# GpSimd's order inside a chunk of phase 2: the sum of x and y2 goes first, the low half of block 6 goes ahead of the rebuilt y

## The chip, the cores and the metric

The kernel runs on one core of a Trainium2 chip. The metric is the device time of one execution in microseconds (us). The kernel before took 651.34 us (median of three runs, 648.35 to 652.54). TensorE is called PE below, VectorE DVE, ScalarE ACT, GpSimd POOL, and the engine that only issues transfers SP.

## The reference, cut to what matters

The input is 8192 rows of 256 numbers (2 sequences of 4096). Two layers follow each other, each behind a layer norm and with a residual.

```
y   = _layernorm(x)
h   = y + linear_attention(_layernorm(y)*g1+b1, wq, wk, wv) @ wo     # y2 in the kernel
h   = h + lookup_act((_layernorm(h)*g2+b2) @ w1) @ w2                # w1: 256x1024, w2: 1024x256
x   = x + h                                                          # xp in the kernel
out = x + (_layernorm(x) @ CB.T) * (SCB/127) + bias
```

lookup_act rounds its argument to steps of 0.1 and takes the GELU of the rounded value.

## The kernel before

The rows are worked off in 16 chunks of 512 (each held as 128 partitions x 4 rows x 256). Phase 1 (up to about 204 us) runs over all chunks and leaves the key-value sums and phi(q). Phase 2 runs over the chunks again and does the rest; the change lies there. Every matmul operand in fp32 is split into a rounded "high" part and a "low" part (the rest), which are multiplied one after the other.

Each engine has its own instruction stream, written by hand, and the streams meet at semaphores. Nothing is scheduled by a tool. In phase 2 each stream is a function `body(i, ...)` that mixes work of neighbouring chunks: `main` is the MLP of chunk i, `prv` what is left of chunk i - 1 (its xp, its norm n3, the product with CB, the output), `nxt` what has to be ready for chunk i + 1 (its attention output, y2, norm n2), `nn` work for chunk i + 2.

What each engine does in a chunk, in the order of its stream:

- PE (`body`, L1133): up 0, up 1 (products with w1, blocks of 128 of the 1024 columns), turn of the attention, up 2, up 3, down 0 (product with w2, needs high and low part of block 0), attention_out (with wo), down 1, up 4, turn of n3 (needs `n3_ready`), down 2, up 5, down 3, up 6, the product with CB, turn of n2 (`turn2`, needs `n2_ready`), up 7, down 4, the first half of the attention of chunk i + 2, down 5, down 6, its second half, down 7.
- ACT (`body`, L556): for each block of up a rounding to int8 (L540), GELU into `tf` (L548) and GELU into the high part `t_hi` (L550, signals `t_hi_ready`). Between them the high parts of the turned tiles (L494 and L503). The GELU of block m waits until the low part of block m - 2 has read `tf`.
- DVE (`body`, L772): xp = PSUM + xz (L778), the statistics of xp (L615), low part of the attention (L745), mean and variance (L622), low part of block 1 (L738), n3 (`normalise`, four instructions at L729), low of block 3, y2 of chunk i + 1 (L755), its statistics, the low part of turned n3 (L745), n2 of chunk i + 1 (L729 again), ot (L802), low of block 5 (L738), low part of turned n2 (L768), attention of chunk i + 2 first half (L712 to L719), low of block 7 (L738), second half of the attention.
- POOL (`body`, L345): low parts of the even blocks (`mlp_low`, one instruction at L343, signals `t_lo_p`), the powers for n3 and n2 (`power`, L322 and L324), xz = x + y2 of chunk i (L355, waits for `xp_ready` of chunk i - 1 since xp reads the old xz), y of chunk i + 2 rebuilt from x (`first_norm`, L330 and four at L336), xb = xp + bias (L367) and the output ot + xb (L372).

SP reads x of chunk i + 2 once xz of chunk i is done (`xz_ready`), and writes an output once `out_ready` says so.

Of the kernel before, what the change touches and what calls it, by code (L numbers as in the profile page):

```python
# [24 lines left out]
ALU = mybir.AluOpType  # L25
# [19 lines left out]
def wait(eng, sem, value):  # L45

    if isinstance(value, int) and value <= 0:
        return
    eng.wait_ge(sem, value)
# [8 lines left out]
def build(nc, x, ln1_g, ln1_b, wq, wk, wv, wo, ln2_g, ln2_b, w1, w2, cb, scb, bias, out):  # L58
# [15 lines left out]
    with ctx:  # L74
# [3 lines left out]
        def sem(name):  # L78
            return ctx.enter_context(nc.semaphore(name))
# [57 lines left out]
        x2 = [take(CE) for _ in range(2)]  # L137
        take(CE)
        xz, xp, xb, ot = (take(CE) for _ in range(4))
# [3 lines left out]
        yb, at_, y2, nt = (take(CE) for _ in range(4))  # L143
# [44 lines left out]
        s = {n: sem(n) for n in names}  # L188
# [9 lines left out]
        def tm(a):  # L198

            return a.rearrange("p (j d) -> p j d", j=TT)  # L200
# [71 lines left out]
        def _(g):  # L272
# [46 lines left out]
            def power(c, u, r, mv, ready, arg, done):  # L319
                wait(g, s[ready], c + 1)  # L320
                hold(g, s["held_pool"])
                nc.gpsimd.tensor_scalar(u[:, :], mv[:, 1:2 * TT:2], 1.0, EPS, ALU.mult, ALU.add).then_inc(s[arg], 1)  # L322
                g.wait_ge(s[arg], c + 1)
                nc.gpsimd.tensor_tensor(r[:, :], u[:, :], minus_half[:, 0:TT], ALU.pow).then_inc(s[done], 1)  # L324

            def first_norm(c, p, turn):

                wait(g, s["y_ready"], c)
                hold(g, s["held_pool"])
                nc.gpsimd.tensor_copy(st2[:, :], chunk(stats_all, c, 2 * TT)).then_inc(s["stats_now"], 1)  # L330
                g.wait_ge(s["stats_now"], c + 1)
                g.wait_ge(x2_loaded[p], turn * 16 + 16)
                wait(g, s["y2_ready"], c)
                hold(g, s["held_pool"])
                for j in range(TT):
                    i = nc.gpsimd.tensor_scalar(tm(yb)[:, j], tm(x2[p])[:, j], st2[:, j:j + 1], st2[:, TT + j:TT + j + 1],  # L336
                                                ALU.mult, ALU.add)
                i.then_inc(s["y_ready"], 1)

            def mlp_low(c, m):  # L340
                n = c * (MT // 2) + m // 2
                wait(g, s["t_hi_ready"], c * MT + (m + 1))
                nc.gpsimd.tensor_tensor(t_lo[m % SLOTS], tf[m % 2], t_hi[m % SLOTS].bitcast(F32), ALU.subtract).then_inc(s["t_lo_p"], 1)  # L343

            def body(i, p, turn, prv, main, nxt, nn):  # L345

                if main:
                    mlp_low(i, 0)
                if prv:
                    power(i - 1, u3, r3, mv3, "mv3_ready", "u3_ready", "pow3")  # L350
                if main:

                    wait(g, s["xp_ready"], i)
                    g.wait_ge(s["y2_ready"], i + 1)
                    nc.gpsimd.tensor_tensor(xz, x2[p], y2, ALU.add).then_inc(s["xz_ready"], 1)  # L355
                    mlp_low(i, 2)
                if nxt:
                    power(i + 1, u2, r2, mv2, "mv2_ready", "u2_ready", "pow2")
                if main:
                    mlp_low(i, 4)  # L360
                if nn:
                    first_norm(i + 2, p, turn + 1)
                if main:
                    mlp_low(i, 6)
                if prv:
                    wait(g, stored, i * 16)
                    nc.gpsimd.tensor_tensor(tm(xb), tm(xp), bias_b.unsqueeze(1).to_broadcast([P, TT, D]),  # L367
                                            ALU.add).then_inc(s["xb_ready"], 1)
                if prv:
                    g.wait_ge(s["ot_ready"], i + 2)  # L370
                    g.wait_ge(s["xb_ready"], i + 2)
                    nc.gpsimd.tensor_tensor(xb, ot, xb, ALU.add).then_inc(s["out_ready"], 1)  # L372
# [23 lines left out]
            nc.gpsimd.tensor_scalar(scb_b, scb_b, 1.0 / 127.0, 0.0, ALU.mult, ALU.add).then_inc(s["scb_scaled"], 1)  # L396
            g.wait_ge(loaded["bias"], 16)
            body(0, 0, 0, False, True, True, True)
            body(1, 1, 0, True, True, True, True)
            with g.Fori(1, CHUNKS // 2 - 1) as it:  # L400
                for p in range(2):
                    body(it * 2 + p, p, it, True, True, True, True)
# [868 lines left out]
```

## Time and profile before

| | |
|---|---|
| median of three runs | 651.34 us |
| the profiled execution, its own time | 651.4 us |
| its span, first to last instruction | 649.6 us |
| outside the span | 1.8 us |
| phase 2 begins (chunk 0's first products) | about 204 us |
| xp of chunk 0 to xp of chunk 13 (13 chunks) | 227.27 to 582.47 us |
| DVE, ACT, POOL busy over the span | 80%, 63%, 59% |
| mean of one ACT instruction at L540, L548, L550 | 681, 632, 619 ns |

Times in the trace are counted from the start of the span. A row of the timeline gives the start, the length, the engine, the line, what is written from what, how many instructions are merged into the row, and in brackets how long the engine sat idle just before and what ended that. A chunk is followed below from the start of DVE's xp (L778), called xp + 0. PE's matmul ends are modelled, so starts are the better marks on PE.

### The profile page before, as it was taken

How to read it: one execution, taken by the hardware profiler on the slowest of the kernel's cores; microseconds unless marked ns; L12 is line 12 of the kernel's file. 1: busy time of each engine (PE TensorE's matmuls, PEld its weight loads, DVE VectorE, ACT ScalarE, POOL GpSimd, SP SyncE). 2: the span in 40 equal slices, each digit the busy share in tenths (PEclk: the TensorE clock that was granted, in tenths of full speed). 3: DMA queues.
4: the chain of work that ended last, by engine and by line, in shares of the span. 5: the costliest groups of instructions: out<-in, count | busy, mean ns of one | idle time of the engine just before them, and what ended most of it. 6: DMA issues, size and time to landing. Idle time of an engine off the chain costs nothing.

```text
span 649.6 us, 12205 instructions
## 1 busy us (share of the span) xinstructions
PE 586.2 (90%) x3838; PEld 517.6 (80%) x3838; DVE 517.0 (80%) x1076; ACT 411.7 (63%) x767; POOL 386.2 (59%) x337
## 2 busy tenths in 40 slices
PE   6999999999997999898998989989899898998875
PEld 6887787878786878788787978879788797887675
DVE  5488988898873688878888788887988878888656
ACT  2377767676765685675756757576665766657560
POOL 3446475655542447676486765757657576675553
PEclk8599999999997999999999999999999999999898
DMA  8101112021101000000100001010110000100001
GB/s 287 53 34 65 59 38 65 32 65 34 66 1 36 17 32 33 32 32 32 65 32 32 33 33 65 32 32 32 32 65 32 32 32 32 65 24 11 33 1 67
DMA packets 11128, 29.16 MB, mean 45 GB/s; under 512 B 2016, under 2 KB 4576, under 8 KB 11104
## 3 DMA queue, kind: packets, MB, share of 16 engines
q1 hardware_dynamic: 9472, 28.32, 12.3%
q10 hardware_dynamic: 1632, 0.53, 0.4%
q8 instruction: 15, 0.25, 0.2%
q14 instruction: 9, 0.07, 0.0%
HBM read 20.45 MB, written 8.39 MB: 44 GB/s over the span
## 4 chain that ended last, share of the span: by engine, by line
PE 36%; DVE 27%; issue 16%; POOL 12%; ACT 6%; DMA 1%; DVEq 1%; ACTq 0%; POOLq 0%; SPq 0%
PE psum L914 31%; DVE f_arena L729 8%; POOL f_arena L355 5%; DVE bn_stats L615 5%; PE psum L932 4%; POOL rstd L324 3%; DVE f_arena L755 3%; DVE f_arena L657 2%; DVE mean_var L622 2%; ACT grid_index L540 2%; DVE f32r_arena L738 2%; POOL pow_arg L322 2%; ACT f32r_arena L550 2%; ACT f32r_arena L494 1%; DVE f_arena L642 1%
## 5 line engine op out<-in xcount | busy, mean ns | idle before, releaser
L914 PE MATMUL psum<-w_hi,f32r_arena 128*128 128x256 f32 x1280 | 178.7, 286 | 5.1 <-DVE f32r_arena L738 3.5
L914 PEld LDWEIGHTS psum<-w_hi,f32r_arena 128*128 128x128 f32 x1280 | 164.9, 190 | 16.0 <-issue 11.5
L914 PE MATMUL psum<-f32r_arena,w_hi 128*128 128x512 f32 x512 | 143.0, 411 | 3.7 <-issue 3.7
L540 ACT ACTIVATE grid_index<-psum,w_bias_in_steps 128x512 int8<-128x512 f32 x128 | 87.2, 681 | 69.9 <-PE psum L914 69.9
L729 DVE TENSOR_SCALAR f_arena<-f_arena,mean_var,rstd 128x256 f32<-128x256 f32 x124 | 102.7, 887 | 25.9 <-POOL rstd L324 25.9
L914 PE MATMUL psum<-f32r_arena 128*128 128x512 f32 (+1 forms) x512 | 120.5, 378 | 2.6 <-issue 1.5
L343 POOL TENSOR_TENSOR f32r_arena<-f_arena,f32r_arena 128x512 fp32r<-128x512 f32 x64 | 86.0, 1344 | 56.3 <-ACT f32r_arena L550 56.3
L914 PEld LDWEIGHTS psum<-f32r_arena,w_hi 128*128 128x128 f32 x512 | 91.1, 194 | 22.4 <-ACT grid_index L540 4.7
L932 PE MATMUL psum<-ident,f_arena 128*128 128x128 f32 x504 | 69.6, 283 | 36.9 <-DVE f_arena L729 32.3
L932 PEld LDWEIGHTS psum<-ident,f_arena 128*128 128x128 f32 x504 | 58.6, 145 | 52.1 <-issue 28.3
L914 PEld LDWEIGHTS psum<-f32r_arena 128*128 128x128 f32 x512 | 83.2, 190 | 14.9 <-issue 3.1
L548 ACT ACTIVATE f_arena<-grid_index 128x512 f32<-128x512 int8 x128 | 80.9, 632 | 16.0 <-POOL f32r_arena L343 10.7
L550 ACT ACTIVATE f32r_arena<-grid_index 128x512 fp32r<-128x512 int8 x128 | 79.2, 619 | 0.0
L322 POOL TENSOR_SCALAR pow_arg<-mean_var 128x4 f32<-128x4 f32 x31 | 10.4, 334 | 97.5 <-DVE mean_var L622 97.4
L657 DVE SCALAR_TENSOR_TENSOR f_arena<-f_arena 128x256 f32<-128x256 f32 x64 | 46.4, 733 | 18.4 <-ACT f_arena L473 17.8
L738 DVE TENSOR_TENSOR f32r_arena<-f_arena,f32r_arena 128x512 fp32r<-128x512 f32 x64 | 51.8, 810 | 7.4 <-ACT f32r_arena L550 7.4
L745 DVE TENSOR_TENSOR f32r_arena<-psum,f32r_arena 128x512 fp32r<-128x512 f32 x62 | 39.5, 679 | 22.3 <-ACT f32r_arena L494 22.3
L494 ACT ACTIVATE f32r_arena<-psum 128x512 fp32r<-128x512 f32 x62 | 33.5, 595 | 31.9 <-PE psum L932 31.9
L285 POOL TENSOR_SCALAR pow_arg<-mean_var 128x4 f32<-128x4 f32 x16 | 8.3, 520 | 69.4 <-DVE mean_var L622 69.4
L615 DVE BATCH_NORM_STATS2 bn_stats<-f_arena 128x6 f32<-128x256 f32 x128 | 44.9, 414 | 4.7 <-DMA f_arena<-in_L_attn_x_dram 4.2
L914 PEld LDWEIGHTS psum<-f_arena 128*128 128x128 f32 x260 | 36.2, 192 | 15.6 <-DVE f_arena L657 12.9
L914 PE MATMUL psum<-f_arena 128*128 128x129 f32 (+1 forms) x260 | 41.6, 288 | 5.5 <-DVE f_arena L657 4.8
(96 smaller groups left out, 976.4 us busy)
## 6 DMA issues: line engine op xcount, KB each, us to landing
f_arena<-in_L_attn_x_dram SPq DMA_DIRECT2D x32, 512.0 KB, 3.3
out_dram<-f_arena SPq DMA_DIRECT2D x15, 512.0 KB, 2.6
f_arena<-in_L_attn_w_dram SPq DMA_DIRECT2D x2, 1024.0 KB, 11.3
out_dram<-f_arena SPq DMA_DIRECT2D x2, 256.0 KB, 2.2
phi_q<-in_L_attn_wk_dram ACTq DMA_DIRECT2D x1, 256.0 KB, 4.9
phi_q<-in_L_attn_wv_dram ACTq DMA_DIRECT2D x1, 256.0 KB, 5.4
phi_q<-in_L_attn_wq_dram SPq DMA_DIRECT2D x1, 256.0 KB, 5.7
phi_q<-in_L_ffn_CB_dram SPq DMA_DIRECT2D x1, 256.0 KB, 7.8
```

Of the source, the lines that this page charges most:

```text
L343: nc.gpsimd.tensor_tensor(t_lo[m % SLOTS], tf[m % 2], t_hi[m % SLOTS].bitcast(F32), ALU.subtract).then_inc(s["t_lo_p"], 1)
L494: act(fm(dst)[:, k], bank(b + k), ACT.Copy).then_inc(s[done], 1)
L540: act(k8[:, m % 2], bank(AB + m % 2), ACT.Identity, scale=1.0 / STEP, bias=h_bias[:, m:m + 1]).then_inc(s["grid_ready"], 1)
L548: act(tf[m % 2], k8[:, m % 2], ACT.Gelu_apprx_tanh, scale=STEP)
L550: act(t_hi[m % SLOTS], k8[:, m % 2], ACT.Gelu_apprx_tanh, scale=STEP).then_inc(s["t_hi_ready"], 1)
L615: i = ve.bn_stats(scratch[:, 6 * j:6 * j + 6], tm(src)[:, j])
L657: ve.scalar_tensor_tensor(out=phi_k[j], in0=e_k[j % 2], scalar=1.0, in1=relu_k[j % 2], op0=ALU.min, op1=ALU.add).then_inc(s["phi_k_done"], 1)
L729: i = ve.tensor_scalar(tm(nt)[:, j], tm(src)[:, j], mv[:, 2 * j:2 * j + 1], r[:, j:j + 1], ALU.subtract, ALU.mult)
L738: ve.tensor_tensor(t_lo[m % SLOTS], tf[m % 2], t_hi[m % SLOTS].bitcast(F32), ALU.subtract).then_inc(s["t_lo_v"], 1)
L745: ve.tensor_tensor(fm(lo_)[:, k], bank(b + k), fm(hi_)[:, k].bitcast(F32), ALU.subtract).then_inc(s[done], 1)
L914: return nc.tensor.matmul(out_, lhs, rhs, start=start, stop=stop, skip_group_check=True)
L932: i = nc.tensor.transpose(bank(b + k)[:, j * P:(j + 1) * P], tm(src)[:, j, k * P:(k + 1) * P], ident[:, :])
```

## The change

Only POOL's stream in phase 2 changes, and only in the order of its instructions. No instruction is added or taken away, no operand and no semaphore is changed.

- xz of chunk i moves from behind the power of n3 to the head of the chunk, in front of the low part of block 0. It keeps its wait for xp of chunk i - 1 (`xp_ready`), so the low part of block 0 and the power of n3 now stand behind that wait.
- The low part of block 6 moves ahead of `first_norm(i + 2)`, which keeps its own waits. The low parts of blocks 4 and 6 now follow each other.
- The power of n3 is followed by the low part of block 2, where it was followed by xz.

```
             def body(i, p, turn, prv, main, nxt, nn):
                 if main:
+                    wait(g, s["xp_ready"], i)
+                    g.wait_ge(s["y2_ready"], i + 1)
+                    nc.gpsimd.tensor_tensor(xz, x2[p], y2, ALU.add).then_inc(s["xz_ready"], 1)
                     mlp_low(i, 0)
                 if prv:
                     power(i - 1, u3, r3, mv3, "mv3_ready", "u3_ready", "pow3")
                 if main:
-                    wait(g, s["xp_ready"], i)
-                    g.wait_ge(s["y2_ready"], i + 1)
-                    nc.gpsimd.tensor_tensor(xz, x2[p], y2, ALU.add).then_inc(s["xz_ready"], 1)
                     mlp_low(i, 2)
                 if nxt:
                     power(i + 1, u2, r2, mv2, "mv2_ready", "u2_ready", "pow2")
                 if main:
                     mlp_low(i, 4)
+                if main:
+                    mlp_low(i, 6)
                 if nn:
                     first_norm(i + 2, p, turn + 1)
-                if main:
-                    mlp_low(i, 6)
```

Place 1 is POOL at the head of the loop over chunks. `f32r_arena<-f_arena,f32r_arena 128x512` is a low part, `f_arena<-f_arena 128x1024` at L355 or L351 is xz, and the two rows with `pow_arg` are the power of n3.

```order
 L400 ISA
+L350 REGISTER_ALU [waits xp_ready]
+L351 TENSOR_TENSOR f_arena<-f_arena 128x1024 [waits y2_ready]
+L49 ISA
 L343 TENSOR_TENSOR f32r_arena<-f_arena,f32r_arena 128x512 [waits t_hi_ready]
 L322 TENSOR_SCALAR pow_arg<-mean_var 128x4 [waits mv3_ready]
 L324 TENSOR_TENSOR rstd<-pow_arg,minus_half 128x4 [waits u3_ready]
-L354 REGISTER_ALU [waits xp_ready]
-L355 TENSOR_TENSOR f_arena<-f_arena 128x1024 [waits y2_ready]
 L49 REGISTER_ALU
 L343 TENSOR_TENSOR f32r_arena<-f_arena,f32r_arena 128x512 [waits t_hi_ready]
```

xz with its two waits has moved over block 0's low part and over the power.

Place 2 is the second half of the same chunk on POOL, from block 4's low part to the output. Before:

```order
L343 TENSOR_TENSOR f32r_arena<-f_arena,f32r_arena 128x512 [waits t_hi_ready]
L330 ISA [waits y_ready]
L330 COPY ln_scale_shift_now<-ln_scale_shift 128x8
L331 REGISTER_ALU
L332 ISA [waits stats_now]
L336 TENSOR_SCALAR f_arena<-f_arena,ln_scale_shift_now 128x256 [waits loaded_x2_0,y2_ready]
L336 TENSOR_SCALAR f_arena<-f_arena,ln_scale_shift_now 128x256 x3
L49 REGISTER_ALU
L343 TENSOR_TENSOR f32r_arena<-f_arena,f32r_arena 128x512 [waits t_hi_ready]
L49 REGISTER_ALU
L367 TENSOR_TENSOR f_arena<-f_arena 128x1024 [waits stored]
L372 TENSOR_TENSOR f_arena<-f_arena 128x1024 [waits xb_ready,ot_ready]
```

The same place now:

```order
L343 TENSOR_TENSOR f32r_arena<-f_arena,f32r_arena 128x512 [waits t_hi_ready]
L49 REGISTER_ALU
L343 TENSOR_TENSOR f32r_arena<-f_arena,f32r_arena 128x512 [waits t_hi_ready]
L330 ISA [waits y_ready]
L330 COPY ln_scale_shift_now<-ln_scale_shift 128x8
L331 REGISTER_ALU
L332 ISA [waits stats_now]
L336 TENSOR_SCALAR f_arena<-f_arena,ln_scale_shift_now 128x256 [waits loaded_x2_0,y2_ready]
L336 TENSOR_SCALAR f_arena<-f_arena,ln_scale_shift_now 128x256 x3
L49 REGISTER_ALU
L367 TENSOR_TENSOR f_arena<-f_arena 128x1024 [waits stored]
L372 TENSOR_TENSOR f_arena<-f_arena 128x1024 [waits xb_ready,ot_ready]
```

The second low part (block 6) has moved over the copy and the four instructions of y; xb (L367) now follows y directly.

## Rows read from the trace of the kernel before

**Rows 1.** The page, engines: busy us, share of the span, instructions.
```profile
PE 586.2 (90%) x3838; PEld 517.6 (80%) x3838; DVE 517.0 (80%) x1076; ACT 411.7 (63%) x767; POOL 386.2 (59%) x337
```

**Rows 2.** Windows, 13 chunks: stretch, length, busy and count by engine, clock, DMA.
```profile
227.27:582.47 355.20, 326.70 (x2290) 293.35 (x2289) 296.72 (x586) 235.21 (x403) 237.37 (x208) 1.00 0.10 37
```

**Rows 3.** Waits, 228 to 592 us: who waited, for whom, sum, times, longest.
```profile
PE psum L932 <- DVE f_arena L729: 27.6, 26, 1.6
```

**Rows 4.** Timeline of PE in one chunk, 337 to 365 us.
```profile
340.80 1.11 PE L914 MATMUL psum<-w_hi,f32r_arena 128*128 128x256 f32 x8
...
348.17 1.09 PE L932 MATMUL psum<-ident,f_arena 128*128 128x128 f32 x8 [1.54 <-DVE f_arena L729]
...
355.87 1.09 PE L932 MATMUL psum<-ident,f_arena 128*128 128x128 f32 x8 [0.66 <-DVE f_arena L729]
...
362.32 1.19 PE L914 MATMUL psum<-w_hi,f32r_arena 128*128 128x256 f32 x8
```

**Rows 5.** Timeline of DVE in the same chunk.
```profile
336.46 1.22 DVE L778 TENSOR_TENSOR f_arena<-psum,f_arena 128x1024 f32<-128x1024 f32 x1
337.71 1.41 DVE L615 BATCH_NORM_STATS2 bn_stats_b<-f_arena 128x6 f32<-128x256 f32 x4
...
341.42 0.37 DVE L622 BATCH_NORM_AGGREGATE mean_var<-bn_stats_b 128x2 f32<-128x6 f32 x4
...
343.70 4.34 DVE L729 TENSOR_SCALAR f_arena<-f_arena,mean_var,rstd 128x256 f32<-128x256 f32 x4 [1.27 <-POOL rstd L324]
...
353.37 2.44 DVE L729 TENSOR_SCALAR f_arena<-f_arena,mean_var,rstd 128x256 f32<-128x256 f32 x4 [0.45 <-POOL rstd L324]
...
361.25 0.68 DVE L738 TENSOR_TENSOR f32r_arena<-f_arena,f32r_arena 128x512 fp32r<-128x512 f32 x1
```

**Rows 6.** Timeline of POOL in the same chunk.
```profile
339.19 1.29 POOL L343 TENSOR_TENSOR f32r_arena<-f_arena,f32r_arena 128x512 fp32r<-128x512 f32 x1 [2.08 <-ACT f32r_arena L550]
341.99 0.50 POOL L322 TENSOR_SCALAR pow_arg<-mean_var 128x4 f32<-128x4 f32 x1 [1.50 <-DVE mean_var L622]
342.57 1.02 POOL L324 TENSOR_TENSOR rstd<-pow_arg,minus_half 128x4 f32<-128x4 f32 x1
343.56 2.39 POOL L355 TENSOR_TENSOR f_arena<-f_arena 128x1024 f32<-128x1024 f32 x1
345.91 1.33 POOL L343 TENSOR_TENSOR f32r_arena<-f_arena,f32r_arena 128x512 fp32r<-128x512 f32 x1
...
353.23 1.29 POOL L343 TENSOR_TENSOR f32r_arena<-f_arena,f32r_arena 128x512 fp32r<-128x512 f32 x1
...
354.96 2.36 POOL L336 TENSOR_SCALAR f_arena<-f_arena,ln_scale_shift_now 128x256 f32<-128x256 f32 x4 [0.24 <-POOL ln_scale_shift_now L330]
...
358.97 2.40 POOL L367 TENSOR_TENSOR f_arena<-f_arena 128x1024 f32<-128x1024 f32 x1
```

**Rows 7.** Timeline of ACT in the same chunk: block 2's high part, block 6's rounding.
```profile
342.93 0.61 ACT L550 ACTIVATE f32r_arena<-grid_index 128x512 fp32r<-128x512 int8 x1
...
353.14 0.67 ACT L540 ACTIVATE grid_index<-psum,w_bias_in_steps 128x512 int8<-128x512 f32 x1
```

**Rows 8.** Timeline, POOL, DVE and PE at the end of chunk 14.
```profile
606.17 2.35 POOL L372 TENSOR_TENSOR f_arena<-f_arena 128x1024 f32<-128x1024 f32 x1
606.94 2.12 DVE L738 TENSOR_TENSOR f32r_arena<-f_arena,f32r_arena 128x512 fp32r<-128x512 f32 x1 [0.93 <-ACT f32r_arena L550]
609.21 1.26 PE L914 MATMUL psum<-w_hi,f32r_arena 128*128 128x256 f32 x8 [2.57 <-DVE f32r_arena L738]
610.51 1.23 DVE L778 TENSOR_TENSOR f_arena<-psum,f_arena 128x1024 f32<-128x1024 f32 x1 [1.45 <-PE psum L914]
```

**Rows 9.** Timeline of PE in chunk 15, the turn of n3.
```profile
621.32 1.09 PE L932 MATMUL psum<-ident,f_arena 128*128 128x128 f32 x8 [2.48 <-DVE f_arena L729]
```

**Rows 10.** Lines L615 and L802, 228 to 595 us: count, shortest/median/longest ns.
```profile
L615 DVE BATCH_NORM_STATS2 bn_stats_b<-f_arena x56: 408/410/428, 228.5 to 584.7; 128x6 f32<-128x256 f32 x56
L802 DVE TENSOR_TENSOR f_arena<-psum,f_arena x13: 1205/1206/1214, 246.5 to 574.3; 128x1024 f32<-128x1024 f32 x13
```

More of the change, by code:

```diff
@@ L347, in body @@
                 if main:
+                    wait(g, s["xp_ready"], i)
+                    g.wait_ge(s["y2_ready"], i + 1)
+                    nc.gpsimd.tensor_tensor(xz, x2[p], y2, ALU.add).then_inc(s["xz_ready"], 1)
                     mlp_low(i, 0)
@@ L351, in body @@
                 if main:
-                    wait(g, s["xp_ready"], i)
-                    g.wait_ge(s["y2_ready"], i + 1)
-                    nc.gpsimd.tensor_tensor(xz, x2[p], y2, ALU.add).then_inc(s["xz_ready"], 1)
                     mlp_low(i, 2)
@@ L360, in body @@
                     mlp_low(i, 4)
+                if main:
+                    mlp_low(i, 6)
                 if nn:
                     first_norm(i + 2, p, turn + 1)
-                if main:
-                    mlp_low(i, 6)
                 if prv:
```

## The prediction

> **What bounds the kernel now.** I read the engines on the page first: PE is busy 90% of the span and no other engine over 80% [rows 1]. The windows view gives the repeating part. From xp of chunk 0 to xp of chunk 13 it takes 355.20 us for 13 chunks, 27.32 us each, at a granted clock of 1.00 [rows 2]. PE is busy 326.70 / 13 = 25.13 of those 27.32, so some 2.2 us a chunk are there to be won from it. The waits view says where they are: PE's turns of normalised tiles wait for DVE's normalise (L729) 27.6 us in 26 waits [rows 3]. In one chunk these are 1.54 us ahead of the turn of n3 and 0.66 us ahead of that of n2 [rows 4].
>
> The first is made by POOL. DVE's four instructions of n3 take 4.34 us, those of n2 2.44 us, for the same work on the same shapes [rows 5]. n3 starts at 343.70, when POOL has been in xz (2.39 us) for 0.14 us, and behind xz comes block 2's low part (1.33 us) [rows 6]. n2 starts 0.14 us into a low part of 1.29 us [rows 5, 6] and loses only about that. So a `normalise` instruction does not run while a POOL instruction does; it waits for its end. Chunk 14 shows the same for DVE's low part (L738). Block 7's starts at 606.94, 0.77 us into POOL's output instruction, which ends at 608.52, and ends itself at 609.06, 0.54 later; it takes 2.12 us [rows 8] where it takes 0.68 in the steady chunk [rows 5]. PE waits 2.57 us for it [rows 8].
>
> **The change, step by step.** All times from xp + 0 = 336.46.
>
> *Head of the chunk.* xp ends at 1.22 [rows 5]. POOL follows a DVE signal after about 0.2 (L622 ends 341.79, L322 starts 341.99) [rows 5, 6], so xz runs 1.42 to 3.8. Its old cover is gone: block 0's low part, which ran from 2.73 (339.19), now runs 3.8 to 5.1. PE's down 0 started at 4.34 (340.80) [rows 4]; with 0.1 for the signal it starts at 5.2. **Cost: 0.86 us of PE.** Behind down 0 on PE stands everything up to down 7. The power of n3 is not delayed: it waits for L622, which is ready at 5.33, and it started at 5.53 anyway [rows 5, 6].
>
> *n3.* The power ends at 7.13 [rows 6]. Block 2's high part is there at 7.08 (342.93 + 0.61) [rows 7], so the low part of block 2 runs from about 7.15 to 8.45, and n3 starts into it 0.1 us after its start. That is exactly the case of n2: 2.44 us in place of 4.34. n3 ends at 9.7 in place of 11.6, **1.9 us earlier**. PE gets to the turn of n3 at 5.83 us after down 0 (348.17 - 1.54 - 340.80) [rows 4], so at 11.0: it no longer waits. DVE's y2, its statistics, the power of n2, block 4's low part and n2 all move up by 1.9: low 4 ends at 16.15 (354.52 before), n2 at 17.45 [rows 5, 6]. PE is at the turn of n2 12.87 us after down 0 (355.87 - 340.80 - 1.54 - 0.66) [rows 4], at 18.1: no wait either. Up to here PE has won 2.20 and paid 0.86, **1.34 us a chunk**.
>
> *Second half.* Block 6's low part stands right behind block 4's, but its high part is not there. ACT rounds block 6 at 16.68 (353.14) [rows 7]; the rounding follows the turn of n3, so it comes 5.2 + (353.14 - 340.80 - 1.54) = 16.0 now. Three ACT instructions of 0.68, 0.63 and 0.62 us later it is 17.9. POOL waits from 16.15 and runs low 6 from 17.9 to 19.25. Then y: from the end of low 4 (354.52) to the end of L336 (357.32) it took 2.8 us [rows 6]. DVE's low part of block 5 asks for its turn at about 19.2 too; if it gets in first, POOL starts 0.6 later. So y ends at 22.05 to 22.65 and xb (2.40) at 24.45 to 25.05. Before, xb ended at 361.37, 24.9: the 1.9 us won by n3 are spent waiting for block 6.
>
> *What is late next.* Block 7's low part on DVE started at 361.25 [rows 5], 20.45 us after down 0; without the two PE waits 18.25, so it now starts at 5.2 + 18.25 = 23.45. That is inside xb. Before, it came 0.12 us ahead of xb's end and lost nothing. Now it waits for xb's end and takes 0.54 more, as in chunk 14: it ends at 25.0 to 25.6. PE, which would be ready for down 7 at 5.2 + (362.32 - 340.80 - 2.20) = 24.5 [rows 4], starts it 0.15 after that (609.06 to 609.21), at 25.15 to 25.75. The next xp comes 1.30 after down 7 (609.21 to 610.51) [rows 8]: the chunk takes 26.45 to 27.05 us. I take the middle, **26.75, or 0.57 us less a chunk**. POOL's output instruction then ends near 27.6, 0.9 behind the next xp and ahead of the 1.42 at which the next xz could start, so it adds nothing.
>
> Here a rule can be set beside the rows. The Trainium skill, page "SBUF — State Buffer", section "Who interferes with whom", says that a DVE instruction with two SBUF inputs contends with a GpSimd instruction that reads SBUF, and that who issues first holds the shared ports for the whole instruction. By that rule L738 pays for xb in full, as the row of 606.94 has it; without it the chunk would take the 25.8 of the first rival.
>
> *The ends.* Chunk 0 has no n3; I take nothing there. In chunk 14 there is no y, so xb starts at 19.25 to 19.85 and the output ends near 24.0 to 24.6; block 7's low part then ends at 24.5 to 25.1 and down 7 starts at 24.7 to 25.3 behind that chunk's xp (582.47), before at 26.74 [rows 8]: 1.4 to 2.0, take 1.6. In chunk 15 the turn of n3 waits 2.48 us [rows 9], because POOL stood at block 0's low part with xz still to come; with xz done while it waits, n3 loses one short instruction: 1.9 of the 2.48.
>
> *Transfers.* The read of x for chunk i + 2 hangs on xz and starts some 6 us earlier, the write of the output where it did. Nothing waits for either.
>
> **Sum.** 13 x 0.57 = 7.4, plus 1.6, plus 1.9: 10.9 us. The profiled execution took 651.4 us (span 649.6 and 1.8 around it), the median of three runs is 651.34: there is no difference to carry over. 651.4 - 10.9 = **640.5 us**. With 26.45 and 27.05 us a chunk and both ends of chunk 14 it is 636 to 645.
>
> **Rivals.**
>
> 1. *Block 7's low part escapes xb.* This happens if POOL's y ends later than 23.45 (0.8 to 1.4 us later than worked out), or if block 7's low part does not wait for an xb already running. Then down 7 starts at 24.5, the next xp at 25.8, and 13 x 1.52 = 19.8 plus 3.5 give **628 us**. Against it stands the row of 606.94. Chance 0.15.
>
> 2. *All is given back at xb.* y took 2.8 us in the chunk shown; every instruction of it that meets DVE adds up to 0.55. With 0.5 us more there and low 5 first, y ends at 23.15, xb at 25.55, and the chunk takes 25.55 + 0.54 + 0.15 + 1.30 = 27.5. 13 x 0.2 us are lost against 3.5 won at the ends: **650.5 us**, no change. Chance 0.2.
>
> 3. *Slower: xz and the statistics of xp get into each other's way.* xz now runs from 1.42, over DVE's L615 (337.71 to 339.12, four instructions) [rows 5]. If these wait like L729 does, one waits for xz (2.4) and one for low 0 (1.3). The two L745 behind them move from 3.75 to some 5.9, the attention's low part is there at 7.2 where PE wants it at 6.1, and mean and variance at 7.5. Everything from attention_out on is 1.2 later, the chunk takes 27.95, and the ends win 1.2 less each: 651.4 + 8.2 - 1.1 = **658.5 us**. It decides from the point at which down 0 and what follows are 0.6 later than worked out. Against it: L615 takes 408 to 428 ns in all 56 cases, but none of those had POOL beside it, so it is a gap and no proof. The nearest case, L802, reads one SBUF tile and PSUM while POOL is in y, and takes 1205 to 1214 ns throughout [rows 10]. Chance 0.08.
>
> For the third rival the same page and section of the Trainium skill has a rule: a DVE instruction with at most one SBUF input and outside the two-port modes does not contend with GpSimd. L802 agrees with it; for L615 no run here shows it yet. By the rule the third rival costs nothing and the 640.5 stand.
>
> **How the numbers follow.** The forecast (26.45 to 27.05 us a chunk, 636 to 645) has 0.52, the rivals 0.15, 0.2 and 0.08, and 0.05 is left for what I have not seen. The range takes in the first two rivals and leaves out the third: 626 to 651 us. A difference under 1% (644.9 to 657.9) can hardly be told from no change by a measurement of this kernel. Faster by over 1%: the forecast but for its upper edge (0.49), the first rival and a little of the rest, 0.66. Within 1%: 0.24. Slower: 0.1.
>
> **What the profile after would show.** Right: the first L729 row of a chunk takes 2.44 in place of 4.34; PE has no wait ahead of the turn of n3, but 0.6 us ahead of down 0 for POOL's L343, and 1 us or so ahead of down 7 for DVE's L738; that L738 takes 1.5 to 2.2 us; POOL waits 1.7 us for ACT ahead of block 6's low part. Wrong: if L738 stays at 0.68 there (first rival), if L615 grows beyond 0.43 (third), or if down 0 starts later than 5.3 behind xp. The forecast also falls if the order of PE's waits is not what I think, above all if n2 is late after all.

## The result and the profile after

| | before | changed |
|---|---|---|
| median | 650.99 us (4 runs, 648.35 to 652.54) | 633.17 us (4 runs, 631.93 to 634.82) |
| ratio | | 0.973, 95% interval 0.969 to 0.977 |
| span of the profiled execution | 649.6 us | 632.0 us |
| xp of chunk 0 | 227.27 | 223.34 |
| 13 chunks, xp 0 to xp 13 | 355.20 us, 27.32 each | 343.39 us, 26.41 each |
| chunk 14, xp to xp | 28.04 us | 26.96 us |
| from xp of chunk 14 to the end | 39.10 us | 38.34 us |

The kernel is 17.8 us faster; 10.9 were forecast. 633.2 us lies inside the stated range of 626 to 651 us, but below the 636 to 645 us of the forecast itself. Of the 17.6 us between the two profiled spans 11.8 lie in the 13 chunks, 1.1 in chunk 14, 0.8 behind it, and 3.9 ahead of the first xp, where the change touches almost nothing.

These are the rows of the changed kernel that answer to [rows 4 to 7]; the chunk shown begins with xp at 328.99. First PE: down 0, the turns of n3 and n2, down 7.

```profile
333.99 1.23 PE L914 MATMUL psum<-w_hi,f32r_arena 128*128 128x256 f32 x8 [0.38 <-POOL f32r_arena L343]
...
339.82 1.03 PE L932 MATMUL psum<-ident,f_arena 128*128 128x128 f32 x8
...
346.35 1.09 PE L932 MATMUL psum<-ident,f_arena 128*128 128x128 f32 x8
...
354.10 1.19 PE L914 MATMUL psum<-w_hi,f32r_arena 128*128 128x256 f32 x8 [1.04 <-DVE f32r_arena L738]
```

Both waits ahead of the turns are gone. Two others stand there: 0.38 us ahead of down 0 and 1.04 us ahead of down 7. DVE in the same chunk: xp, n3, n2, the low part of block 7, the next xp.

```profile
328.99 1.23 DVE L778 TENSOR_TENSOR f_arena<-psum,f_arena 128x1024 f32<-128x1024 f32 x1 [0.19 <-PE psum L914]
...
336.36 2.34 DVE L729 TENSOR_SCALAR f_arena<-f_arena,mean_var,rstd 128x256 f32<-128x256 f32 x4 [1.27 <-POOL rstd L324]
...
344.01 2.28 DVE L729 TENSOR_SCALAR f_arena<-f_arena,mean_var,rstd 128x256 f32<-128x256 f32 x4 [0.43 <-POOL rstd L324]
...
351.73 2.23 DVE L738 TENSOR_TENSOR f32r_arena<-f_arena,f32r_arena 128x512 fp32r<-128x512 f32 x1
...
355.42 1.22 DVE L778 TENSOR_TENSOR f_arena<-psum,f_arena 128x1024 f32<-128x1024 f32 x1 [0.18 <-PE psum L914]
```

n3 takes 2.34 us in place of 4.34, and block 7's low part 2.23 in place of 0.68. POOL in the same chunk: xz, low 0, the power of n3, low 2, low 4, low 6, y, xb and the output.

```profile
330.29 2.39 POOL L351 TENSOR_TENSOR f_arena<-f_arena 128x1024 f32<-128x1024 f32 x1 [0.52 <-DVE f_arena L778]
332.64 1.29 POOL L343 TENSOR_TENSOR f32r_arena<-f_arena,f32r_arena 128x512 fp32r<-128x512 f32 x1
...
335.24 1.02 POOL L324 TENSOR_TENSOR rstd<-pow_arg,minus_half 128x4 f32<-128x4 f32 x1
336.28 1.29 POOL L343 TENSOR_TENSOR f32r_arena<-f_arena,f32r_arena 128x512 fp32r<-128x512 f32 x1
...
343.87 1.30 POOL L343 TENSOR_TENSOR f32r_arena<-f_arena,f32r_arena 128x512 fp32r<-128x512 f32 x1
346.75 1.29 POOL L343 TENSOR_TENSOR f32r_arena<-f_arena,f32r_arena 128x512 fp32r<-128x512 f32 x1 [1.59 <-ACT f32r_arena L550]
...
348.88 2.18 POOL L336 TENSOR_SCALAR f_arena<-f_arena,ln_scale_shift_now 128x256 f32<-128x256 f32 x4 [0.24 <-POOL ln_scale_shift_now L330]
351.03 2.38 POOL L367 TENSOR_TENSOR f_arena<-f_arena 128x1024 f32<-128x1024 f32 x1
353.56 2.66 POOL L372 TENSOR_TENSOR f_arena<-f_arena 128x1024 f32<-128x1024 f32 x1
```

Block 7's low part asks at 351.73, 0.70 us into xb, which ends at 353.41; it ends itself at 353.96, 0.55 later. The waits view over 228 to 580 us says the same of all chunks (13 or 14 of each), where [rows 3] stood before:

```profile
PE psum L914 <- DVE f32r_arena L738: 13.4, 13, 1.2
...
PE psum L914 <- POOL f32r_arena L343: 5.9, 14, 0.6
```

No wait of PE's turns for L729 is left on PE's own row.

### The profile page after: what moved, and what is told of

The parts are those of the page before. It is cut to its first block, busy times and chain, and to the rows that moved or that the text cites. A ratio compares the mean times of both kernels' runs of the same rounds, so it can differ in the third digit from the quotient of the medians.

```text
span 632.0 us, 12211 instructions
## 1 busy us (share of the span) xinstructions
PE 579.8 (92%) x3838; PEld 514.7 (81%) x3838; DVE 504.9 (80%) x1076; ACT 411.3 (65%) x767; POOL 380.4 (60%) x337
## 4 chain that ended last, share of the span: by engine, by line
PE 37%; DVE 23%; POOL 17%; issue 15%; ACT 5%; DMA 1%; DVEq 1%; POOLq 0%; ACTq 0%; SPq 0%
PE psum L914 32%; PE psum L932 5%; DVE f32r_arena L738 4%; POOL f_arena L351 3%; DVE bn_stats L615 3%; POOL f32r_arena L343 3%; DVE f_arena L657 3%; POOL f_arena L372 3%; POOL f_arena L367 2%; DVE f_arena L729 2%; DVE f_arena L642 2%; POOL f_arena L336 2%; DVE f32r_arena L768 2%; POOL rstd L324 2%; DVE f_arena L755 1%
## 5 line engine op out<-in xcount | busy, mean ns | idle before, releaser
L914 PEld LDWEIGHTS psum<-f32r_arena,w_hi 128*128 128x128 f32 x512 | 89.6, 191 | 23.3 <-ACT grid_index L540 5.5
L343 POOL TENSOR_TENSOR f32r_arena<-f_arena,f32r_arena 128x512 fp32r<-128x512 f32 x64 | 83.0, 1297 | 35.9 <-ACT f32r_arena L550 35.4
L729 DVE TENSOR_SCALAR f_arena<-f_arena,mean_var,rstd 128x256 f32<-128x256 f32 x124 | 71.2, 634 | 25.7 <-POOL rstd L324 25.7
L738 DVE TENSOR_TENSOR f32r_arena<-f_arena,f32r_arena 128x512 fp32r<-128x512 f32 x64 | 69.1, 1080 | 7.5 <-ACT f32r_arena L550 7.4
L932 PEld LDWEIGHTS psum<-ident,f_arena 128*128 128x128 f32 x504 | 59.6, 145 | 14.8 <-DVE f_arena L642 3.9
L657 DVE SCALAR_TENSOR_TENSOR f_arena<-f_arena 128x256 f32<-128x256 f32 x64 | 49.3, 780 | 14.3 <-ACT f_arena L473 13.7
L745 DVE TENSOR_TENSOR f32r_arena<-psum,f32r_arena 128x512 fp32r<-128x512 f32 x62 | 39.5, 679 | 24.1 <-ACT f32r_arena L494 24.1
L615 DVE BATCH_NORM_STATS2 bn_stats<-f_arena 128x6 f32<-128x256 f32 x128 | 44.9, 413 | 4.8 <-DMA f_arena<-in_L_attn_x_dram 4.3
L351 POOL TENSOR_TENSOR f_arena<-f_arena 128x1024 f32<-128x1024 f32 x16 | 38.2, 2389 | 16.1 <-DVE f_arena L778 14.9
```

What stands on the lines that cost most here:

```text
L615: i = ve.bn_stats(scratch[:, 6 * j:6 * j + 6], tm(src)[:, j])
L657: ve.scalar_tensor_tensor(out=phi_k[j], in0=e_k[j % 2], scalar=1.0, in1=relu_k[j % 2], op0=ALU.min, op1=ALU.add).then_inc(s["phi_k_done"], 1)
L729: i = ve.tensor_scalar(tm(nt)[:, j], tm(src)[:, j], mv[:, 2 * j:2 * j + 1], r[:, j:j + 1], ALU.subtract, ALU.mult)
L738: ve.tensor_tensor(t_lo[m % SLOTS], tf[m % 2], t_hi[m % SLOTS].bitcast(F32), ALU.subtract).then_inc(s["t_lo_v"], 1)
L745: ve.tensor_tensor(fm(lo_)[:, k], bank(b + k), fm(hi_)[:, k].bitcast(F32), ALU.subtract).then_inc(s[done], 1)
L914: return nc.tensor.matmul(out_, lhs, rhs, start=start, stop=stop, skip_group_check=True)
```

## The experiments

Each line of an experiment's kernel stands one or two lower or higher than in the changed kernel (L777 or L779 is xp, L737 or L739 the low part on DVE, L728 or L730 n3 and n2, L349 xz where it stands at the head). Times per chunk are from xp of chunk 0 to xp of chunk 13 in the profiled execution, divided by 13. e1 to e4 ran on one chip, e5 to e8 on a second, e9 to e11 on a third. POOL's order in a chunk, in short:

| kernel | POOL's order | us a chunk | median us |
|---|---|---|---|
| before | low0 pow3 **xz** low2 pow2 low4 y low6 xb out | 27.32 | 651 |
| changed | xz low0 pow3 low2 pow2 low4 **low6 y** xb out | 26.41 | 633.2 |
| e1 | xz low0 pow3 low2 pow2 low4 y low6 xb out | 25.52 | 620.4 |
| e2 | low0 pow3 xz low2 pow2 low4 low6 y xb out | 28.16 | 661.0 |
| e3 | xz low0 pow3 low2 pow2 low4 low6 xb y out | 25.79 | 625.2 |
| e5 | low0 xz pow3 low2 pow2 low4 y low6 xb out | 26.19 | 632.5 |
| e7 | xz low0 pow3 low2 (n3) xb pow2 low4 low6 out y | 25.35 | 618.2 |
| e8 | low0 xz pow3 low2 (n3) xb pow2 low4 low6 out y | 26.09 | 629.5 |
| e9 | as e7 without the wait for n3 | 27.28 | 649.5 |

"(n3)" is a wait for DVE's n3.

### The two halves apart

e1_xz_only takes the move of block 6's low part back out of the changed kernel:

```
                     mlp_low(i, 4)
-                if main:
-                    mlp_low(i, 6)
                 if nn:
                     first_norm(i + 2, p, turn + 1)
+                if main:
+                    mlp_low(i, 6)
```

> Half of the change: xz at the head of the chunk, the low part of block 6 back behind y (first_norm). Theory A (a VectorE instruction with two SBUF inputs waits for the GpSimd instruction that is running, so block 7's low part pays for xb): with y right behind block 4's low part (16.2 us behind xp) y ends at 19.0, low 6 at 20.3, xb at 22.7 to 23.1. Block 7's low part asks at 22.7, so it loses at most 0.4 us where the changed kernel lost 1.5 (2.23 us in place of 0.68). PE's wait of 1.04 us ahead of down 7 goes, a chunk takes 25.4 to 25.7 in place of 26.43, 13 chunks win 10 to 13 us: 620 to 624 us. Rival B (the tail of the chunk is set by PE's own work and the wait at down 0, and block 6's low part is needed early): PE waits for the late low 6 ahead of down 6 instead, a chunk takes 26.4 or more, 633 us or above.

Measured: 620.4 us (618.22 to 625.84), 13 us less than the changed kernel. All 13 chunks took 25.3 to 25.5 us but one of 27.28. PE has no wait for L737 in the others. So this half alone brings more than both together, and the move of low 6 costs 13 us (10 us by the second measurement of e1's kernel, below).

The one slow chunk begins at 374.59. Of its end, first POOL (low 6, xb, output), then DVE (low 5, low 7):

```profile
393.29 1.29 POOL L343 TENSOR_TENSOR f32r_arena<-f_arena,f32r_arena 128x512 fp32r<-128x512 f32 x1
394.53 2.85 POOL L366 TENSOR_TENSOR f_arena<-f_arena 128x1024 f32<-128x1024 f32 x1
397.53 2.34 POOL L371 TENSOR_TENSOR f_arena<-f_arena 128x1024 f32<-128x1024 f32 x1
```

```profile
393.25 1.88 DVE L737 TENSOR_TENSOR f32r_arena<-f_arena,f32r_arena 128x512 fp32r<-128x512 f32 x1
...
397.64 2.78 DVE L737 TENSOR_TENSOR f32r_arena<-f_arena,f32r_arena 128x512 fp32r<-128x512 f32 x1
```

Low 5 begins 0.04 us ahead of low 6, and yet DVE waits here for POOL's whole low 6. Low 7 then comes 0.11 us behind the start of the output and waits for the rest of its 2.34 us. In the chunk ahead the same two met the other way round (low 5 at 367.91 took 0.79, POOL's low 6 from 368.13 took 1.72), and low 7 took 0.86. In the other 25 chunks (13 in each of this kernel's two profiles) low 5 was 0.06 us or more ahead and went first: a few hundredths of a microsecond decide over 1.9 us.

e2_low6_only keeps that move and puts xz back behind the power of n3:

```
                 if main:
-                    wait(g, s["xp_ready"], i)
-                    g.wait_ge(s["y2_ready"], i + 1)
-                    nc.gpsimd.tensor_tensor(xz, x2[p], y2, ALU.add).then_inc(s["xz_ready"], 1)
                     mlp_low(i, 0)
                 if prv:
                     power(i - 1, u3, r3, mv3, "mv3_ready", "u3_ready", "pow3")
+                if main:
+                    wait(g, s["xp_ready"], i)
+                    g.wait_ge(s["y2_ready"], i + 1)
+                    nc.gpsimd.tensor_tensor(xz, x2[p], y2, ALU.add).then_inc(s["xz_ready"], 1)
                 if main:
                     mlp_low(i, 2)
```

> The other half: block 6's low part ahead of y, xz where it was before (behind the power of n3). Theory A: n3 still takes 4.34 us behind xz and low 2, low 4 ends at 18.1 behind xp, low 6 waits for its high part and ends at 20.6, y at 23.4 to 24.0, xb at 25.8 to 26.4. Block 7's low part asks at 24.8, waits for xb and ends at 26.3 to 26.9; a chunk takes 27.8 to 28.4 in place of 27.32: 657 to 665 us, slower than before. Rival B: the earlier low 6 costs nothing and saves nothing, 27.3 us a chunk, 651 us.

Measured: 661.0 us, ratio to before 1.016 (1.010 to 1.022); 28.16 us a chunk. Slower than before by 1 to 2%, as theory A had it. DVE, n3 and the low part of block 7:

```profile
343.46 4.35 DVE L728 TENSOR_SCALAR f_arena<-f_arena,mean_var,rstd 128x256 f32<-128x256 f32 x4 [1.26 <-POOL rstd L324]
...
360.85 1.91 DVE L737 TENSOR_TENSOR f32r_arena<-f_arena,f32r_arena 128x512 fp32r<-128x512 f32 x1
```

n3 is back at 4.35 with xz behind the power, and block 7's low part pays for xb (359.83 to 362.22) with xz in either place. The two halves of the change act nearly apart: xz at the head is worth 27.32 - 25.35 = 1.97 us a chunk with the old tail (e1's undisturbed chunks) and 28.16 - 26.41 = 1.75 with the new one, and low 6 ahead of y costs 0.84 (28.16 - 27.32) in one order and 1.06 (26.41 - 25.35) in the other.

### Other instructions under block 7's low part

e3_xb_first swaps xb and y in the changed kernel:

```
                     mlp_low(i, 6)
+                if prv:
+                    wait(g, stored, i * 16)
+                    nc.gpsimd.tensor_tensor(tm(xb), tm(xp), bias_b.unsqueeze(1).to_broadcast([P, TT, D]),
+                                            ALU.add).then_inc(s["xb_ready"], 1)
                 if nn:
                     first_norm(i + 2, p, turn + 1)
-                if prv:
-                    wait(g, stored, i * 16)
-                    nc.gpsimd.tensor_tensor(tm(xb), tm(xp), bias_b.unsqueeze(1).to_broadcast([P, TT, D]),
-                                            ALU.add).then_inc(s["xb_ready"], 1)
```

> The changed kernel with xb (= xp + bias, 2.4 us, one instruction) moved ahead of y (a copy and four instructions of 0.55 us): the same work, only shorter instructions run on GpSimd when block 7's low part asks. Theory A: low 6 ends at 19.05 behind xp, xb at 21.45, y at 24.2, block 7's low part asks at 22.7 and loses at most 0.57: it ends near 23.9, down 7 starts at PE's own pace (24.07), a chunk takes 25.4 to 25.6, 620 to 622 us. If the output, which now ends near 26.9, or 1.4 us behind the next xp, holds up the next xz, 0.1 to 0.3 less is won. Rival B: no gain, 26.4 us a chunk, 633 us.

Measured: 625.2 us, 25.79 us a chunk; 8 us less than the changed kernel. In the 13 chunks low 7 now meets only the four short instructions of y and took at most 0.74 us; PE does not wait for it. The gain is 0.62 a chunk and not the 0.8 to 1.0 expected, since the output now comes last, which the expectation had as a condition. POOL across the border of a chunk (xp at 350.16): y, the output, xz, low 0; then PE's down 0.

```profile
347.03 2.63 POOL L336 TENSOR_SCALAR f_arena<-f_arena,ln_scale_shift_now 128x256 f32<-128x256 f32 x4 [0.24 <-POOL ln_scale_shift_now L330]
349.63 2.40 POOL L371 TENSOR_TENSOR f_arena<-f_arena 128x1024 f32<-128x1024 f32 x1
351.98 2.39 POOL L349 TENSOR_TENSOR f_arena<-f_arena 128x1024 f32<-128x1024 f32 x1
354.32 1.28 POOL L343 TENSOR_TENSOR f32r_arena<-f_arena,f32r_arena 128x512 fp32r<-128x512 f32 x1
```

```profile
355.66 1.21 PE L913 MATMUL psum<-w_hi,f32r_arena 128*128 128x256 f32 x8 [1.11 <-POOL f32r_arena L343]
```

xz follows the output without a gap and starts 1.82 us behind xp in place of 1.30; down 0 waits 1.11 us. POOL is full at the border here: what ends later in the tail comes out at down 0.

### Block 0's low part ahead of xz

e5_low0_first is e1 with xz one place later:

```
                 if main:
+                    mlp_low(i, 0)
+                if main:
                     wait(g, s["xp_ready"], i)
                     g.wait_ge(s["y2_ready"], i + 1)
                     nc.gpsimd.tensor_tensor(xz, x2[p], y2, ALU.add).then_inc(s["xz_ready"], 1)
-                if main:
-                    mlp_low(i, 0)
```

> Block 0's low part first again, then xz, then the power of n3; the tail as in e1_xz_only (y, low 6, xb, output). Separates the price of the place of xz from the rest. Theory A: down 0 no longer waits for xz (started 5.0 us behind xp, 0.4 of it a wait), but the power of n3 starts at 6.5 in place of 5.7, n3 ends at 10.5 in place of 9.7 and PE is at its turn at 10.4: the two nearly cancel, a chunk takes 25.1 to 25.4 against 25.35 in the undisturbed chunks of e1_xz_only, 614 to 620 us. Rival B: n3 being later by 0.8 us makes n2 late at its turn (needed at 17.0, ready at 18.3), a chunk takes 26.0 or more, 628 us.

Measured: 632.5 us, 26.19 us a chunk. Theory A's number fell, rival B holds: down 0 has no wait any more, but the power of n3 starts at 6.42 us behind xp in place of 5.43 in e1 and PE waits for both turns again.

```profile
338.49 1.09 PE L931 MATMUL psum<-ident,f_arena 128*128 128x128 f32 x8 [0.44 <-DVE f_arena L728]
...
346.15 1.09 PE L931 MATMUL psum<-ident,f_arena 128*128 128x128 f32 x8 [0.64 <-DVE f_arena L728]
```

In e1 the wait at down 0 was 0.62 us (0.43 in the changed kernel); here the two turns cost 0.44 to 0.64 us each, 1.0 a chunk. So of the two costs of xz's place the one at down 0 is the cheaper.

### xb in POOL's idle stretch, and xb under n3

e7_xb_gap moves xb into the 5.04 us in which POOL waits for n2's mean and variance, behind a wait for n3, and puts the output ahead of y:

```
                     mlp_low(i, 2)
+                if prv:
+                    g.wait_ge(s["n3_ready"], i)
+                if prv:
+                    wait(g, stored, i * 16)
+                    nc.gpsimd.tensor_tensor(tm(xb), tm(xp), bias_b.unsqueeze(1).to_broadcast([P, TT, D]),
+                                            ALU.add).then_inc(s["xb_ready"], 1)
                 if nxt:
                     power(i + 1, u2, r2, mv2, "mv2_ready", "u2_ready", "pow2")
...
                     mlp_low(i, 6)
-                if nn:
-                    first_norm(i + 2, p, turn + 1)
-                if prv:
-                    wait(g, stored, i * 16)
-                    nc.gpsimd.tensor_tensor(tm(xb), tm(xp), bias_b.unsqueeze(1).to_broadcast([P, TT, D]),
-                                            ALU.add).then_inc(s["xb_ready"], 1)
                 if prv:
                     g.wait_ge(s["ot_ready"], i + 2)
                     g.wait_ge(s["xb_ready"], i + 2)
                     nc.gpsimd.tensor_tensor(xb, ot, xb, ALU.add).then_inc(s["out_ready"], 1)
+                if nn:
+                    first_norm(i + 2, p, turn + 1)
```

> xz at the head, xb moved into GpSimd's idle stretch behind n3 (with a wait for n3, so that it cannot lie under it), the output right behind block 6's low part, y last. Theory A: no instruction of 2.4 us is running when VectorE's low part of block 7 asks (22.7 us behind xp; the output runs 19.1 to 21.7, then four short ones), so it loses at most 0.57 and PE never waits for it, in chunks 14 and 15 as well. A chunk takes 25.35 to 25.5, all chunks alike, and the ends win 2 us more: 613 to 617 us. Rival B: xb in the gap delays the power of n2 or y2 and gives it back: 26 us a chunk, 628 us.

Measured: 618.2 us (613.27 to 621.08), ratio to before 0.949 (0.943 to 0.954). All 13 chunks took 25.3 to 25.5 us, chunk 14 24.5 in place of 26.96. The chunks are those of theory A, the time is 1 us above its 613 to 617. DVE in one chunk, n3 and low 7:

```profile
335.18 2.34 DVE L730 TENSOR_SCALAR f_arena<-f_arena,mean_var,rstd 128x256 f32<-128x256 f32 x4 [1.27 <-POOL rstd L324]
...
350.71 0.68 DVE L739 TENSOR_TENSOR f32r_arena<-f_arena,f32r_arena 128x512 fp32r<-128x512 f32 x1
```

Neither waits for a long instruction; what is left of PE's waits is down 0's, 0.62 us.

e8_low0_xb_gap is e7 with block 0's low part ahead of xz.

> As e7_xb_gap, with block 0's low part ahead of xz. Theory A: down 0 saves its wait of 0.4 us and the turn of n3 waits 0.1: 25.0 to 25.3 us a chunk, 609 to 615 us. Rival B: the power of n3, now 0.8 us later, delays n2 (needed by PE at 17.0 behind xp), 25.8 us a chunk or more, 622 us.

Measured: 629.5 us, 26.09 us a chunk. Theory A fell, rival B again: PE waits 0.45 us for n3 and 0.48 for n2. So xz ahead of low 0 is the better place with both tails tried, e1's and e7's.

e9_xb_under_n3 takes only the wait out of e7:

```
                 if prv:
-                    g.wait_ge(s["n3_ready"], i)
-                if prv:
                     wait(g, stored, i * 16)
```

> e7_xb_gap without its wait for n3: xb (2.4 us) stands right behind block 2's low part and so under VectorE's n3, as xz did in the kernel before. Nothing else changes. Theory A (a normalise instruction waits for the GpSimd instruction that is running): the first of the four waits for low 2, the second for xb; n3 takes 4.7 to 4.8 us in place of 2.34, ends at 12.1 behind xp and PE, at its turn at 10.8, waits 1.3 to 1.5 us; n2 is late too (ends at 20, PE at its turn at 18.7). 26.9 to 28.0 us a chunk in place of 25.35, so 20 to 34 us more than e7_xb_gap: 636 to 652 us. Rival B (n3 was slow for its place behind the power, not for what runs beside it): n3 takes 2.3 us and the time is that of e7_xb_gap, 618 us.

Measured: 649.5 us, 27.28 us a chunk: 31 us lost by one wait less (30 against e7's kernel on the same chip). POOL (low 2, xb), then DVE (n3), then PE (the turn):

```profile
343.68 1.29 POOL L343 TENSOR_TENSOR f32r_arena<-f_arena,f32r_arena 128x512 fp32r<-128x512 f32 x1
344.93 2.46 POOL L358 TENSOR_TENSOR f_arena<-f_arena 128x1024 f32<-128x1024 f32 x1
```

```profile
343.75 4.43 DVE L728 TENSOR_SCALAR f_arena<-f_arena,mean_var,rstd 128x256 f32<-128x256 f32 x4 [1.27 <-POOL rstd L324]
```

```profile
348.31 1.09 PE L931 MATMUL psum<-ident,f_arena 128*128 128x128 f32 x8 [0.74 <-DVE f_arena L728]
```

The first of the four instructions waits for low 2 (it takes 1.36 us) and the second for xb (2.50); the last two take 0.40 each. This is the kernel before's long n3 made again with another instruction in xz's place. That the chunk also takes nearly the same time (27.32 before) is in part chance: PE waits 0.74 us for n3, 0.48 for n2 and 0.62 at down 0, where it waited 1.54 and 0.66 for the two turns before. I had expected 4.7 to 4.8 us for n3 and a wait of 1.3 to 1.5 us; n3 took 4.43.

### The same kernels again

> The changed kernel once more, for its phase 1. In the two profiles at hand phase 1 ended 3.7 us earlier with the change (attention's low part of chunk 1 at 203.79 in place of 207.51), though no instruction before that point was changed. If that is chance of one execution, phase 1 of this run ends anywhere between 203 and 208 us and the time is 632 to 637 us. If the program with the change always has it, phase 1 ends at 203.8 again and the time is 633 us.

> The kernel before once more, for its phase 1. Five profiles of kernels with another order in phase 2 have the attention's low part of chunk 1 at 202.0 to 204.0 us, the one profile of before at 207.5. If the 3.7 us are chance of that one execution, it comes at 202 to 204 us here and the whole time is about 648 us; if the kernel before always has it, at 207 us again and the time is 651 us.

> The kernel of e7_xb_gap once more, beside e11_xz_only_again, to tell the two apart. Theory A: all chunks take 25.35 us; 615 to 619 us, the spread being that of phase 1.

> The kernel of e1_xz_only once more. Its chunks took 25.35 us but one, in which block 5's low part on VectorE came a moment behind block 6's on GpSimd and the meeting at the output followed, took 27.28. Theory A: 0 to 4 such chunks in an execution, so 616 to 626 us, a wider spread than e10_xb_gap_again and a median 1 to 4 us above it.

Measured: the changed kernel 633.7 us, 26.40 us a chunk; before 650.8 us, 27.32 a chunk; e7's kernel 619.2 us (615.61 to 621.20); e1's kernel 623.4 us (621.48 to 627.70). (In the slow chunk of e1's first profile low 5 came 0.04 us ahead of low 6 and not behind it, as the rows above show.) The time per chunk repeats to 0.03 us. e1's kernel had no slow chunk in this profile (25.36 a chunk), yet its chunk 14 takes 26.2 us where e7's takes 24.6: there is no y in that chunk, and low 7 meets the output (it takes 2.34 us; in e7 0.69). That is 1.6 of the 4.2 us between their two medians on this chip; the rest was not followed up. e7's is the fastest kernel of this study: 32 us below before and 14 below the changed kernel.

Phase 1 does not repeat. The attention's low part of chunk 1 (L745, the first behind it) came at 207.51 and 206.37 in the two profiles of before, at 203.79 and 203.48 in those of the changed kernel, at 202.68 and 205.41 in the two of e1's kernel, at 207.14 and 206.11 in those of e7's; their phase 1 is the same, and a kernel differs from itself by up to 2.7 us. The windows view of the first 25 us shows PE's granted clock at 0.85 in e1's first profile and 0.74 in its second (a mixture of the clock's two levels, 2.4 and 1.2 GHz). That may be some of it, but e7's second profile has 0.84 there and still comes at 206.11. The chip may be another part: the four profiles of e1 to e4, all on one chip, lie at 202.0 to 204.0, the seven on the two other chips at 203.5 to 208.1, and the second profile of before is not from the first. So how much of the 3.9 us that the changed kernel is ahead at its first xp is chance stays open. Both repeats came out as if the difference went with the kernel, and so do the medians: on the chip of e4 before took 651.95 (7 runs beside it) and the changed kernel 633.69, 18.3 us less, while the chunks, chunk 14 and the end make up 13.7 us in the first pair of profiles and 14.8 in the second.

## Why the prediction was right, and where it was off

**n3.** Forecast 2.44 us, end at 9.7 behind xp; measured 2.34, end at 9.71. e9 shows that it is what runs on POOL beside it (4.43 us under two POOL instructions, 2.34 under one). The rule that the prediction took from the Trainium skill, page "SBUF — State Buffer", section "Who interferes with whom", is that for a DVE instruction with two SBUF inputs, and the trace agrees with it for low 7 (2.23 us under xb, 0.68 without). n3 has one SBUF tensor beside its mean and power. For such a `tensor_scalar` the same section has contention with GpSimd in DVE's two-port modes. No row tells n3's mode: its instructions follow each other 0.32 us apart, those of L615, which read as many elements and do not wait, 0.33. That n3 waits is shown; by which of the section's rules is not.

**Head of the chunk.** Forecast: down 0 at 5.2, cost 0.86. Measured 5.00, so a cost of 0.66. xz started 0.07 us behind xp's end and not 0.2: the 0.2 were read from the hand-over by L622, and another instruction's differs.

**Turns of n3 and n2.** No wait at either, as worked out.

**Low 6.** Forecast 17.9 to 19.25 behind a wait of 1.7 us for ACT; measured 17.76 to 19.05, wait 1.59. y ended at 22.07 (forecast 22.05 to 22.65), 3.02 us behind low 6 (2.8 to 3.4): low 5 came first, and the copy ahead of y took 0.65 us in place of 0.26. xb ended at 24.42 (24.45 to 25.05).

**Low 7 and down 7.** The mechanism and its place are those forecast. Low 7 asked at 22.74 and not at 23.45, because it came 17.74 us behind down 0 and not the 18.25 I had read. 0.23 of that is that I took the modelled end of the product with CB as PE's time to the next instruction (they start 1.91 us apart now, and I counted 2.14). Another 0.23 is a wait of before that I did not see: the product with CB began at 353.07, 1.16 us behind the product ahead of it, where it now begins 0.93 behind. Since low 7 waits for xb's end anyway, this changed nothing. Down 7 started at 25.11 (forecast 25.15 to 25.75) and the next xp 1.32 behind it (1.30).

**Sum.** The term that was mis-sized is the chunk: 26.41 where I took 26.75 and gave 26.45 to 27.05. Of these 0.34 us, 0.2 are low 6, which started 0.14 sooner since down 0 did and took 1.29 us where I had 1.35; 0.08 are y with its copy (3.02 where the middle of my two lengths was 3.1), and 0.05 xb (2.35 from y's end to its own, for 2.40). 13 x 0.34 = 4.4 us of the 6.9 by which the kernel was faster than forecast. 3.9 lie ahead of the first xp, where nothing was forecast: whatever they are, the forecast has no part in them. The ends took 1.6 back.

**The ends.** Chunk 14: down 7 at 24.98 behind xp, inside the forecast 24.7 to 25.3, but the chunk won 1.08 and not 1.6. The windows view tells where it went (stretch, length, busy by engine, granted clock, DMA):

```profile
589.00:591.60 2.60, 0.13 (x2) 0.00 (x0) 2.13 (x1) 0.41 (x1) 2.02 (x1) 1.00 0.00 0
591.60:593.60 2.00, 1.89 (x9) 1.92 (x10) 0.00 (x0) 0.00 (x0) 0.00 (x0) 0.56 0.65 262
```

PE had stood 2.58 us for low 7, and the granted clock of the next 2.0 us is 0.56 (mostly the 1.2 GHz level); down 7 took 1.94 us in place of 1.26. Before, the 1.4 us behind the same wait had 0.85. The wait alone does not bring the clock down: in the second profile of before it was 2.56 us, and the 2.0 us behind it had a granted clock of 1.00 (down 7 took 1.19); in that of the changed kernel it was 2.60, with 0.50 behind it (2.05). Chunk 15's turn of n3 came 1.99 us sooner (8.82 in place of 10.81 behind xp; forecast 1.9) and all products behind it too. 1.3 us of that is missing at the end, where 4.07 us lie between DVE's last instruction and the end of the span (2.77 before). The short stretch belongs to that one profile of before and not to its kernel: in the second pair it is 4.4 us before and 4.7 with the change. There the turn of n3 comes 0.75 us sooner (9.27 for 10.02), and from xp of chunk 14 to the end it is 39.48 us in place of 41.53, 2.05 less.

**The rivals.** The first (low 7 escapes xb) did not happen here, but it is what e1, e3 and e7 make of the kernel, at 25.35 to 25.79 us a chunk where I had 25.8. The second fell: it needed 3.9 us for y and its copy, and they took 3.02. The third fell: L615 takes 405 to 430 ns with xz beside it (408 to 428 in [rows 10]), as the same section of the Trainium skill says of an instruction with at most one SBUF input outside the two-port modes (no row tells its mode).

What the prediction did not ask was which half of the change pays. It named the price of block 6's low part (1.9 us won by n3 are spent waiting for it) without drawing that the order y, low 6 would have kept them.

## What to carry to other kernels

An engine that is 60% busy can set the pace by where its long instructions lie: look at what runs on GpSimd when VectorE starts an instruction that normalises a tile in SBUF or subtracts two of them, and put only short ones there, or a wait. Judge the halves of a reordering apart, since one may eat what the other wins. And when a stall is moved, work out what then stands at the other end of the same chunk, down to the start times; within a few hundredths of a microsecond the order of two rivals can flip.

## What the runs showed of the hardware

- L729 and L738 wait for the end of a POOL instruction that is already running; L738 ends 0.54 to 0.55 us behind it (606.94 before, 351.73 after). The wait works the other way too: POOL's low 6 took 1.72 in place of 1.29 us when low 5 had come first.
- Four L729 in a row do not wait as a group. Between two of them POOL's next instruction can start, and the next L729 waits again (4.43 us under 1.29 and 2.46).
- L615 (bn_stats), L745, L778, L802 and L768, with at most one input tensor in SBUF, kept their lengths to within 0.03 us beside POOL, before and with the change (L802 1205 to 1226 ns, L615 405 to 430).
- Behind a PE wait of 2.6 us at the end of chunk 14 the granted clock of the next 2.0 us was 0.56 and 0.50 in the two profiles of the changed kernel, and down 7 took 1.94 and 2.05 us in place of 1.19 to 1.26. Behind a wait as long it was 1.00 in the second profile of before, and in both of e1's, where the wait was 2.8 us.
